# The MLP's up-projection of 7 of 8 chunk pairs by seven block products instead of eight

## The reference

```python
h = layernorm(x, g2, be2)
h = h * (1.0 + scale_mlp) + shift_mlp
h = jax.nn.gelu(h @ W1 + b1, approximate=False) @ W2 + b2
x = x + gate_mlp * h
```

## Time and profile before

| | us |
|---|---|
| median of the runs | 3702.37 |
| the profiled execution, its own time | 3702.52 |
| its span, first to last instruction | 3700.7 |
| granted TensorE clock, mean | 0.999 |
| TensorE busy in the span | 3663.0 (99%) |
| the MLP's first and last matmul start | 2297.9 and 3688.8 |

### The profile page before, as it was taken

One profiled execution on the slowest core, in us unless ns is written; L12 is line 12 of the kernel. 1 busy time (PEld: TensorE's weight loads), 2 busy tenths in 40 slices (PEclk: granted clock), 3 DMA queues, 4 the chain that ended last, 5 costly groups with the idle time before them and its releaser, 6 DMA issues.

```text
span 3700.7 us, 49858 instructions
## 1 busy us (share of the span) xinstructions
PE 3663.0 (99%) x18206; PEld 2614.3 (71%) x18206; DVE 2423.4 (65%) x4164; ACT 1810.2 (49%) x3276; POOL 1957.6 (53%) x635
## 2 busy tenths in 40 slices
PE   8999999999999999999999999999999999999999
PEld 6788885555656565655656555888888888888887
DVE  6677668888988989888888883333333333434442
ACT  3222225666666767666666675433333333333333
POOL 1000116999999999999999997322222222222221
PEclk9999999999999999999999999999999999999999
DMA  8787776767776777677777855112122121222120
GB/s 287 243 272 243 248 247 140 149 141 163 171 163 149 165 170 160 153 161 175 155 159 161 175 130 154 52 63 72 63 88 76 62 69 60 69 71 80 60 69 23
DMA packets 256879, 509.75 MB, mean 138 GB/s; under 512 B 24722, under 2 KB 92306, under 8 KB 240386
## 3 DMA queue, kind: packets, MB, share of 16 engines
q1 hardware_dynamic: 238492, 374.44, 35.5%
q0 software_dynamic: 18144, 132.13, 17.3%
HBM read 240.04 MB, written 132.28 MB: 101 GB/s over the span
## 4 chain that ended last, share of the span: by engine, by line
PE 92%; POOL 3%; issue 2%; DVE 1%; ACT 1%; DMA 0%; SPq 0%; POOLq 0%; DVEq 0%; ACTq 0%
PE psum L741 12%; PE psum L1304 12%; PE psum L1318 12%; PE psum L600 10%; PE psum L602 10%; PE psum L601 10%; PE psum L2022 6%; PE psum L2018 6%; PE psum L2020 6%; PE psum L1349 4%; POOL probs_round L1583 3%; PE psum L1332 2%; PE psum L750 0%; ACT probs L1450 0%; DMA wt<-in_Wt 0%
## 5 line engine op out<-in xcount | busy, mean ns | idle before, releaser
L1123 DVE TENSOR_REDUCE max_part<-psum 128x1 f32<-128x512 f32 x2048 | 1269.8, 678 | 69.1 <-PE psum L741 68.8
L1583 POOL TENSOR_TENSOR probs_round<-probs_round,probs_round 128x2048 f32<-128x2048 f32 x189 | 887.2, 4694 | 105.3 <-PE psum L1318 87.4
L1304 PE MATMUL psum<-q_stack,k_stack 128*128 128x512 f32 x2048 | 768.7, 401 | 0.7 <-ACT probs L1450 0.5
L741 PE MATMUL psum<-k_stack,q_stack 128*128 128x512 f32 x2048 | 754.8, 399 | 0.7
L2232 DVE TENSOR_TENSOR g_parts<-g_full,g_parts 128x512 fp32r<-128x512 f32 x256 | 219.0, 856 | 772.7 <-ACT g_parts L2082 769.3
L1450 ACT ACTIVATE probs_round<-psum 128x512 f32<-128x512 f32 x1024 | 539.1, 605 | 329.8 <-PE psum L1304 326.8
L1450 ACT ACTIVATE probs<-psum 128x512 f32<-128x512 f32 x1024 | 544.7, 606 | 220.8 <-PE psum L1304 206.6
L2079 ACT ACTIVATE g_full<-psum,cols 128x512 f32<-128x512 f32 x256 | 176.6, 690 | 850.8 <-PE psum L602 850.3
L1583 POOL TENSOR_TENSOR probs_round<-probs_round,probs 128x2048 f32<-128x2048 f32 x124 | 571.4, 4608 | 9.7
L2337 POOL TENSOR_TENSOR y_out<-y_out,rows 128x512 f32<-128x512 f32 x60 | 77.1, 1285 | 872.3 <-DVE y_out L2267 872.3
L741 PEld LDWEIGHTS psum<-k_stack,q_stack 128*128 128x128 f32 x2048 | 383.6, 188 | 187.9 <-DVE max_part L1123 113.4
(11 more groups left out here) (202 smaller groups left out, 4912.7 us busy)
## 6 DMA issues: line engine op xcount, KB each, us to landing
probs<-probs POOLq DMA_DIRECT2D x126, 1024.0 KB, 7.8
qk_parts<-qk_out SPq DMA_DIRECT2D x128, 512.0 KB, 4.4
k_stack<-qk_parts SPq DMA_DIRECT2D x96, 512.0 KB, 6.9
q_stack<-qk_parts SPq DMA_DIRECT2D x192, 256.0 KB, 5.5
v_rows<-v_out SPq DMA_DIRECT2D x64, 256.0 KB, 3.7
v_group<-v_rows SPq DMA_DIRECT2D x32, 512.0 KB, 10.1
gated_attention<-gated SPq DMA_DIRECT2D x64, 256.0 KB, 4.7
x<-in_x SPq DMA_DIRECT2D x16, 1024.0 KB, 5.6
```

What stands on the lines that cost most here:

```text
L741: pe.matmul(psum[:, bank, :], q_stack[u % 3][0:P, h, i * P:(i + 1) * P], k_stack[G % 2][0:P, h, kh * CH:(kh + 1) * CH], start=True, stop=T ...
L1123: dve.reduce_max(max_part[:, n:n + 1], psum[:, TURNS[at.turn][0], :], AX.X).then_inc(dve_smax, 1)
L1304: pe.matmul(psum[:, ST[n % 3], :], k_stack[G % 2][0:P, h, kt * P:(kt + 1) * P], q_stack[u % 3][0:P, h, :], start=True, stop=True).then_inc ...
L1583: pool.tensor_tensor(total[:, :, :], total[:, :, :], probs(u, kt)[:, :, :], ALU.add).then_inc(pool_sum, 1)
```

## The change

Chunks 0 and 1 keep the old way. Chunks 2 to 15 are taken as NR = 7 pairs (index `r`). The up-projection of a pair is seen as a product of 2x2 blocks: W1's column tiles i and i + 8, the two halves of the features, and the pair's two chunks. Strassen's scheme (in the form with few additions) makes it by seven block products instead of eight. One **quad** (index `q`, eight of them per pair, `Q = 8r + q`) makes four hidden tiles: column tiles q and q + 8 of both chunks.

- **The sums of features** (`TERMS`, `dve_mix_first` to `dve_mix_fourth`, `act_term_high`, `dve_term_low`): seven terms of two 128x512 tiles, split into high and low, are made once per pair, while the previous pair's second half runs. They lie in SBUF where W1's pieces lay.
- **The sums of weights**: as W1 no longer lies in SBUF, SyncE loads the two column tiles of each quad again from DRAM (`load_raw`, two DMAs of 256 KB in pieces of 512 bytes). VectorE makes four sums of 128x256 (`dve_weights_sums`), ScalarE the high parts and VectorE the low parts of seven blocks of 128x256 in three groups (`act_weights_high`, `dve_weights_low`).
- **The products** (`pe_sum`): each is 2 x 3 matmuls of 128x512. A quad has seven of them in three banks, with partial sums read out of the banks by ScalarE copies and VectorE adds. Between them stand the down units (8 x 3 matmuls) of the first chunk of the pair.
- **The second chunk's hidden tiles** are finished by gelu in `work`, stored to DRAM (`store_hidden`) and loaded again in the pair's second half (`load_hidden`), in which TensorE does only the second chunk's down-projection (`act_half`, `dve_half`).
- **The chunks ahead**: the residual of the next pair's two chunks is built in `x1[0]` and `xn_mlp` one after the other during the quads, stored to DRAM, and loaded again when its chunk is finished. The feature scaling moves from VectorE to ScalarE. GpSimd's list (`pool_mlp`) has the same operations as before, at other places.

The core of the diff (new functions that only carry data are described above):

```diff
+    NQ = KM // 2
+    NR = (NC - 2) // 2
+    GROUPS = ((0, 3), (3, 5), (5, 7))
+    TERMS = ((0, 0, 0), (1, 0, 2), (2, 0, 0), (4, 1, 0), (3, 0, 0), (5, 1, 2), (6, 0, 2))
+    MIXED = {2: 0, 3: 2, 4: 4, 6: 6}
+    TERMS_READY = (2, 4, 6, 10, 8, 12, 14)
+    LAST_UNITS = ((0, 0), (0, 1), (0, 2), (1, 0), (1, 1), (0, 3), (1, 2), (1, 3))
...
+        def pe_sum(pe, Q, s, bank, block):
+            if Q % NQ == 0:
+                ready = 14 * (Q // NQ) + TERMS_READY[s]
+                pe.wait_ge(act_thi, ready)
+                pe.wait_ge(dve_tlo, ready)
+            for k in range(2):
+                cut = slice(k * P, (k + 1) * P)
+                pe.matmul(psum[:, bank, :], w_hi[:, block, cut], t_hi(s)[:, k, :],
+                          start=s < 3 and k == 0, stop=False, skip_group_check=s > 2)
+                pe.matmul(psum[:, bank, :], w_hi[:, block, cut], t_lo(s)[:, k, :],
+                          start=False, stop=False, skip_group_check=s > 2)
+                i = pe.matmul(psum[:, bank, :], w_lo[:, block, cut], t_hi(s)[:, k, :],
+                              start=False, stop=k == 1, skip_group_check=s > 2)
...
+        def pe_quad(pe, r, q):
+            Q = r * NQ + q
+            n = (2 + 2 * r) * KM + 2 * q
+            X = BANK_X[Q % 2]
+            if Q == 0:
+                pe_down_tile(pe, n - 2)
+            pe.wait_ge(act_whi, 3 * Q + 1)
+            pe.wait_ge(dve_wlo, 3 * Q + 1)
+            if Q >= 2:
+                pe.wait_ge(act_ghi, (2 + 2 * ((Q - 2) // NQ)) * KM + 2 * ((Q - 2) % NQ) + 2)
+            pe_sum(pe, Q, 0, X, 1)
+            if Q == 0:
+                pe.wait_ge(act_ghi, 2 * KM - 1)
+            pe_sum(pe, Q, 1, BANK_W, 2)
+            if Q:
+                pe.wait_ge(dve_out_c, 3 * Q)
+            else:
+                pe.wait_ge(act_ghi, 2 * KM)
+            pe_sum(pe, Q, 2, BANK_Z, 0)
+            if Q:
+                pe_down_unit(pe, n - 2, 0)
+                pe_down_unit(pe, n - 2, 1)
+            pe.wait_ge(act_whi, 3 * Q + 2)
+            pe.wait_ge(dve_wlo, 3 * Q + 2)
+            pe.wait_ge(act_other, 5 * Q + 1)
+            pe_sum(pe, Q, 3, X, 3)
+            if Q:
+                pe_down_unit(pe, n - 2, 2)
+                pe_down_unit(pe, n - 2, 3)
+            pe_down_unit(pe, n - 1, 0)
+            if Q == 0:
+                pe_down_unit(pe, n - 1, 1)
+            pe.wait_ge(act_other, 5 * Q + 3)
+            pe_sum(pe, Q, 4, X, 4)
+            if Q:
+                pe_down_unit(pe, n - 1, 1)
+            pe_down_unit(pe, n - 1, 2)
+            pe_down_unit(pe, n - 1, 3)
+            pe.wait_ge(act_whi, 3 * Q + 3)
+            pe.wait_ge(dve_wlo, 3 * Q + 3)
+            pe.wait_ge(dve_out_c, 3 * Q + 2)
+            pe_sum(pe, Q, 5, BANK_Z, 6)
+            pe_sum(pe, Q, 6, X, 5)
...
+        def act_quad(act, r, q):
...
+            act.wait_ge(pe_sums, 7 * Q + 1)
+            act.wait_ge(dve_glo, n - 1)
+            act.activation(natural(g_full[0][:, :]), permuted(X), ACT.Copy).then_inc(act_other, 1)
...
+            act.wait_ge(dve_out_c, 3 * Q + 1)
+            act.wait_ge(pe_down, (n - 2) * TT)
+            act.activation(g_parts[n % 3][:, 0, :], g_full[0][:, :], ACT.Gelu, bias=low)
+            act.activation(g_full[0][:, :], g_full[0][:, :], ACT.Gelu, bias=low).then_inc(act_ghi, 1)
...
+                act_sqrt_mlp(act, 4 + 2 * r + (q == 5))
...
+        def dve_quad(dve, r, q):
...
+            if q > 1:
+                dve_quad_low(dve, n - 1, g_full[1][:, :])
+            if Q:
+                dve_weights_low(dve, Q, 2)
+            dve_sum_low(dve, Q)
...
+                dve_stats_mlp(dve, ahead + 1, (0, 1))
+            if Q + 1 < NR * NQ:
+                dve_weights_sums(dve, Q + 1)
+
+            dve.wait_ge(pe_sums, 7 * Q + 5)
+            dve.wait_ge(act_other, 5 * Q + 2)
+            dve.tensor_tensor(natural(work[1][:, :]), natural(work[1][:, :]), permuted(X),
+                              ALU.add).then_inc(dve_out_c, 1)
+            if Q + 1 < NR * NQ:
+                dve_weights_low(dve, Q + 1, 0)
...
+            elif q == 3 and more:
+                dve_blocks(dve, ahead, (2, 3))
+            elif q == 6 and more:
+                dve_blocks(dve, ahead + 1, (2, 3))
+            elif q == 2 and more:
+                dve_stats_mlp(dve, ahead, (2, 3))
+                dve_moments_mlp(dve, ahead)
+            elif q == 5 and more:
+                dve_stats_mlp(dve, ahead + 1, (2, 3))
+                dve_moments_mlp(dve, ahead + 1)
+            if Q + 1 < NR * NQ:
+                dve_weights_low(dve, Q + 1, 1)
+
+            dve.wait_ge(pe_sums, 7 * Q + 6)
+            dve.wait_ge(act_other, 5 * Q + 3)
+            dve.tensor_tensor(natural(work[0][:, :]), natural(work[0][:, :]), permuted(BANK_Z),
...
+        def sp_quad(sp, r, q):
...
+            if Q + 1 < NR * NQ:
+                sp.wait_ge(dve_wlo, 3 * Q + 3)
+                load_raw(sp, Q + 1)
...
+            elif q == 6 and more:
+                store_blocks(sp, ahead + 1)
+            elif q == 7 and more:
+                sp.wait_ge(a_x1_out[1], X1_0 + 16 * (r + 2))
+                load_features(sp, ahead + 1)
+            store_hidden(sp, Q, 1)
+            if q == 0 and more:
+                sp.wait_ge(act_thi, 14 * (r + 1))
+                sp.wait_ge(dve_tlo, 14 * (r + 1))
+                load_x_ahead(sp, ahead)
+                load_gated_ahead(sp, ahead)
+            elif q == 3 and more:
+                store_x1(sp, ahead)
+            elif q == 7:
+                load_hidden(sp, r, 0)
+                load_hidden(sp, r, 1)
+            store_hidden(sp, Q, 0)
+            if q == 6 and more:
+                sp.wait_ge(a_blocks[1], BLOCKS0 + 64 * (r + 2))
+                load_features(sp, ahead)
+                store_x1(sp, ahead + 1)
+
+        def sp_half(sp, r):
+            for j in range(2, KM):
+                load_hidden(sp, r, j)
...
+        def pool_mlp(pool, done):
...
+            for r in range(NR):
+                ahead = 4 + 2 * r
+                more = r + 1 < NR
+                if more:
+                    for k in range(4):
+                        pool_ahead_part(pool, ahead, k)
+                for n in range(TT):
+                    pool_finish_third(pool, ahead - 3, n)
+                if more:
+                    pool_bias_row(pool, ahead)
+                    for k in range(4):
+                        pool_ahead_part(pool, ahead + 1, k)
+                    pool_bias_row(pool, ahead + 1)
+                for n in range(TT):
+                    pool_finish_third(pool, ahead - 2, n)
+            for n in range(TT - 1):
```

924 lines of the change are left out of this document (678 added, 246 removed).

## The result

| | before | after |
|---|---|---|
| median of the runs, us | 3702.36 | **3800.85** (3798.93 to 3803.19) |
| span of the profiled execution | 3700.7 | 3798.5 |
| granted TensorE clock, mean | 0.999 | 0.989 |

What follows compares the result with a forecast made beforehand. TensorE, busy 99% of the span, was taken as the bound. Saved matmuls -76, stalls in six pairs +103 and the first quad +8 gave +35 us on 3702.5: 3737 us, range 3650 to 3790.

Steps and rivals of the forecast that it cites:

- the likeliest case: Whole kernel: stalls of 12 to 22 us per pair, so 3705 to 3770 us; chance 0.50.
- 336 matmuls at 0.227: Up-projection: 42 matmuls per quad instead of 48 save 76.2 us, the most the change can give.
- GpSimd's halves, quads 1, 5: GpSimd's residual operations lock out VectorE's two-input operations: S6 4.7 us late in quad 1, 1.6 in quad 5.
- bias row, felt in quads 4, 7: GpSimd's bias row, starting in quads 3 and 6, holds VectorE 4.6 us; 2.8 us lost each, 5.6 per pair.
- square roots, quads 3, 6: Table loads and root between ScalarE's gelus delay the next quad's S4 by 1.0 and 2.1 us, 3.1 per pair.
- weights in quad 7: Next pair's raw weights land late behind block turn, features and x; 2.2 us per pair charged, 4.4 if fully serial.
- first quad: The very first quad's weights load only after chunk 1's last up tile: 8 us once, ends 2 and 12.
- second half: Each pair's second half, 192 matmuls in 43.5 us, has slack for the other engines; charged nothing.
- if the weights overtake, 0. I take 2.2: Quad 7: value taken between fully serial weights, S6 4.4 us late, and weights overtaking the transfers ahead, 0.
- a TensorE that also slows down: Rival: gaps of quads 1 and 7 are followed by 1.2 GHz stretches; with serial weights 41 on top, 3778; chance 0.14.
- Undisturbed quads cost nothing; their margins are 1 to 3 us: Quads without other work going through them lose no TensorE time; S6 there has 1.1 us to spare.
- Waits on TensorE in quads 1, 4, 6, 7: Expected sign in the trace: TensorE waits in these quads and none in quad 0.

Runs made afterwards that it cites:

- Run 2: Changed kernel with the square root of chunks 4 to 15 replaced by a copy, so no table loads: 3780.56 us.
- Edits 1 to 5: Changed kernel with, one at a time: next pair's first weights in the half, 3785.16; no root, 3780.56; GpSimd narrow, 3754.20; GpSimd in pieces, 3792.59; SyncE reordered, 3787.08 us.
- run 5: Changed kernel with SyncE's list reordered in quads 6 and 7: raw weights first, the later chunk's features last and scaled two tiles later: 3787.08 us.
- full candidate: Changed kernel with several edits combined and nothing left out of the computation; the best two measured 3760.55 and 3761.08 us.
- run 6: Changed kernel with VectorE's weight sums behind the addition TensorE needs, and ScalarE's first high parts behind its second gelu: 3899.20 us.
- best candidate: Changed kernel with GpSimd in pieces, roots behind the last gelu, SyncE reordered, turn stores behind the first hidden store, weights in the half: 3760.55 us.
- run 7: Changed kernel with the raw weights' two loads per quad issued from ScalarE's queue, not SyncE's: 3843.77 us.

## Why the prediction was wrong

The direction and nearly all places were right; the size was not: 168.8 us lost instead of 111, and 24.5 to 26.2 in a later pair, where the likeliest case had 12 to 22. The time of 3800.85 lies above that case (3705 to 3770) and above the whole range (3650 to 3790). By its terms, over all pairs:

| step | forecast | measured |
|---|---|---|
| 336 matmuls at 0.227 | -76.2 | span less lost time agrees to 8 us in every profile |
| GpSimd's halves, quads 1, 5 | 28, 10 | 29.2, 11.9 |
| bias row, felt in quads 4, 7 | 17, 17 | 15.9 (quad 4), 11 (S3 and S4 of quad 7) |
| square roots, quads 3, 6 | 6, 13 | 18.5, 14.3 |
| weights in quad 7 | 13 | 41 (S6 and S7) |
| quad 2 | 0 | 11.1 |
| first quad | 8 | 14.7 |
| second half | 0 | 1.3 |
| chunk 1 | 0 | some 6 |
| sum of the lost time, without chunk 1 | 111 | 168.8 |

- **Weights behind the block turn: the largest miss, 28 us.** In the fourth pair the landing was forecast near 17 of quad 7 and came at 15.8. The fully serial lateness was forecast as 4.4; S6 came 5.9 late, of which the bias row's share (forecast 2.8) was 1.6, so 4.3 are left. The step that failed is "if the weights overtake, 0. I take 2.2": they never overtook, and nothing in the trace spoke for it; a value between two ends was a mean of two cases, not a likelihood. Over the six pairs the stops ahead of S6 are 29.0 us, 4.8 a pair, and the slower matmuls behind them, 5 to 13 after each, are 12.1: the 41.
- **The clock, left out of the sum.** The rival "a TensorE that also slows down" gave 41 us on top for quads 1 and 7 with serial weights: 3778. What it described happened, and it was the nearest of all the cases. Its 27.6 us of slow matmuls stand beside 29.1 measured, which is luck in part: it put all of them into quads 1 and 7, where 15.0 were, and left the rest of the stage without any. The clock was kept out because no row of the kernel before showed a gap in this stage; that bounds nothing, and its cost should have stood in the sum with a lower end of 0.
- **Square roots: quad 3.** Forecast 1.0, measured 3.1 a pair, of which 2.2 are the stop and 0.9 the slower matmuls behind it. The copy was forecast to end at 6.3 and ended at 7.4 (3114.06 less 3106.62), as forecast for the other quad: both are the late case. Run 2 shows that the roots were all of it.
- **Quad 2, charged nothing.** 8.7 of its 11.1 us are ahead of S6, where the margin was 1.1. Two scalings of the finished chunk (1.41 us) and the exclusion between GpSimd's row additions and the first two weight sums (2.51 us instead of 0.84) stand ahead of VectorE's addition. The prediction charges GpSimd's halves and bias row and calls its short rows harmless for the second half alone; the two rows in quad 2 are in no term. By the last pair, where S6 was 0.5 us late, this takes the margin, and the rest needs a chunk ahead. It is read from timelines; no run took these rows away.
- **First quad.** 14.7 lost, not 8, and above the upper end of 12: 7.6 us of wait for the weights' low part, nine slow matmuls behind it, and S6 late again.
- **GpSimd was right in its places**, and its price only in part. In quad 1 28 us were forecast and 29.2 came, but the stops are 21.0 of them and the rest is slower matmuls and short waits, which this term didn't hold: the fit is luck. Taking the work away gave 46.6 us and not the 71 of its terms: what it covers comes up behind it.
- **"Undisturbed quads cost nothing; their margins are 1 to 3 us"** was right for quad 0 of the later pairs and for the last pair, which lost 0.5 us in all, and small margins are why no edit pays in full. Edits 1 to 5 took 39, 31, 60, 43 and 38 us out of the places that they aimed at, and 16, 20, 47, 8 and 14 out of the time. "Waits on TensorE in quads 1, 4, 6, 7" was too few: quads 2, 3 and 5 had them too.

What stays open: whether quad 7's place in the list is the very last charge, and so whether a version exists that is faster than the kernel before. No version run here is. Also open is what run 5's order is worth when the feature sums aren't late with it: 10 to 17 us at tiles 8 to 11 were in every full candidate that kept this order.

## What to carry to other kernels

When a saving on the busiest engine is paid for with work on engines that stand in its loop, count the slack of each wait and not the idle share: here VectorE went from 38% to 66% busy, and in the pairs whose quads also carried work for the next pair, seven of the eight lost time. A gap on TensorE can have two prices, the gap and the slow matmuls behind it. And where a term can only be serial or overlapped, take the end that the order of the list gives, not the middle. Before moving work behind the instruction that someone waits for, look for the idle time it stood in: in quad 0 the sums that seemed in the way had filled a wait of 4.7 us, and moving them, with ScalarE's high parts, cost 98 us. And look at all that an edit moves: run 5 was meant to try an order of transfers, and most of what came back was VectorE's list.

## What the runs showed of the hardware

- In the kernel after, each of the 9 starts that came over 3.5 us behind the one before was followed by 5 to 13 matmuls 0.40 to 0.47 us apart, then 0.227 again; of the 20 that came 2.0 to 3.5 us behind, 8 were, and of 28 shorter ones (0.65 to 2.0) one. At 299 slow matmuls (run 6) the cost was 59.7 us, at 146 (after) 29.1, at 45 (best candidate) 9.0. The candidate has more matmul distances over 0.6 us than the change (83 against 60), but fewer over 2 us (13 against 29): here many short gaps cost less clock than few long ones.
- GpSimd in pieces of 128x256 needs 7.41 us for what took 5.63, and lets VectorE through in between: the mean of VectorE's 111 low parts of weights of 128x512, over all quads, fell from 1272 to 837 ns.
- Two 256 KB loads from a second queue took 10 us to land beside 2 MB of the first queue, against a median of 3.1 over the kernel (run 7).
